# Scan increments from TensorE through diagonal matrices, C rows by DMA, and a staggered end

## The chip, the cores and the metric

The kernel runs on one core of one Trainium2 chip. The metric is the device time of one execution in microseconds (us). Before the change it is 890.41 us, the median of 3 runs (889.49 to 891.13).

## What is computed

Two layers on 4 sequences of 512 tokens and 128 channels. Each layer is an adaptively normalised pair (layer norm, scale and shift from a condition vector, gate on the way back) of an attention part and a feed-forward part. Layer 0 has an additive attention and a feed-forward part with 4-bit block quantisation of activations and weights (width 352). Layer 1 has two stacked state-space (Mamba) layers and a mixture of 8 experts in which each expert picks its tokens. The change lies mostly in the Mamba part:

```python
def _selective_scan(u, dt, A, Bm, Cm, Dvec):
    dA = jnp.exp(dt[..., None] * A)
    dBu = dt[..., None] * Bm[:, :, None, :] * u[..., None]
    def step(h, xs):
        dA_t, dBu_t, C_t = xs
        h = dA_t * h + dBu_t
        y = jnp.einsum('bdn,bn->bd', h, C_t)
        return (h, y)
    ...
    return jnp.swapaxes(ys, 0, 1) + u * Dvec
def _mamba_layer(x, W_in, conv_w, conv_b, W_x, W_dt, b_dt, A_log, Dvec, W_out):
    u, z = jnp.split(jnp.einsum('bld,ed->ble', x, W_in), 2, axis=-1)
    u = _silu(_causal_conv1d(u, conv_w, conv_b))
    dt, Bm, Cm = jnp.split(jnp.einsum('bld,rd->blr', u, W_x), [DT_RANK, DT_RANK + D_STATE], axis=-1)
    dt = jax.nn.softplus(jnp.einsum('blr,dr->bld', dt, W_dt) + b_dt)
    y = _selective_scan(u, dt, -jnp.exp(A_log), Bm, Cm, Dvec) * _silu(z)
    return jnp.einsum('bld,od->blo', y, W_out)
```

Inner width 256 (two chunks of 128 partitions, IC = 2), 16 states (NS), 4 batches (B), 2 Mamba layers (L), all in float32.

## The kernel before

Each engine runs its own program; semaphores order them. Channels lie on the partitions and time along the free dimension, so one scan instruction runs 512 time steps of 2 x 128 channels for one state. The stages in order: attention; the quantised feed-forward part, in 8 pairs of token tiles; layer norm; then for each of the two Mamba layers l a prologue (projection in, convolution, projections to B, C and dt, softplus) and the loop over batches b and states n; back transposition, gate, layer norm and router; the experts.

In the loop, step n of batch b goes through five engines:

- TensorE spreads the C row to all partitions by a matmul with a selecting matrix (`row_sel` times `bc_parts`, the rows as three bf16 parts, L1064), and the B row likewise: into bank `BB` for the 11 states of `NORMAL` (L1075), and three steps ahead into bank `CB` for the 5 states of `SHARE` (L1081).
- ScalarE copies the C row to `c_row` (L766), the B row of a `SHARE` state to `b_row` (L775), and makes the decay exp(dt A) in two activations (L769).
- VectorE multiplies dt u (`dtuT`) by the B row into PSUM for `NORMAL` states (L1453); GpSimd does so into `dbu` for `SHARE` states (L482).
- VectorE scans (L1468): decay times state plus increment.
- GpSimd multiplies the states by the C row (L495) into one of four buffers of `hc`.
- TensorE adds that to the output in banks 0 and 1, as two f32 matmuls with the identity (`add_state`, L1045), three steps behind (`LAG`). Step 8 adds the skip u D (`add_skip`, L1039); step 5 of the next batch projects out (`project_out`, L1051, in layer 1 with the residual, L1055), and ScalarE stores (`store_h`, L756). VectorE gates the output at step 2 of the next batch (`gate_y`, L1441).

Batch 0 is written out and holds the softplus of batches 1 to 3 (L694, L698, L1399) and dt times u (L457); batches 1 to 3 are a hardware loop (`turns`). A f32 matmul is two records of TensorE (MATMUL x2, each with its LDWEIGHTS); a f32 transposition is one.

In the prologue the projection L1030 gives B, C and dt's low rank rows for one batch; L709, L1409, L726, L467 and L468 split B and C in three bf16 parts; L1017 projects dt; L1418 and L737 prepare the softplus.

In the quantised part each pair is divided by its block scales on GpSimd (L394), its magnitude taken on ScalarE (L566), rounded on VectorE in two passes (`round_fp4`, L1264 and L1265), rescaled on GpSimd (L401), transposed (L957) and multiplied (L967); L946 makes gate and up projections.

The end of the last Mamba layer runs one after the other: projection, four times four back transpositions (L1109), gate and addition (L1475, L1479), statistics of all 16 tiles (L1238, L1241), one square root (L786), normalising on VectorE (L1247), transpositions (L1117), modulation (L789), router matmuls (L1122), and the maximum over experts (L1487).

## Time and profile before

| | |
|---|---|
| median of 3 runs | 890.41 us (889.49 to 891.13) |
| the profiled execution | 889.99 us, of which the span from first to last instruction is 888.2 us |
| mean granted TensorE clock | 0.868 of full |
| busy: TensorE, weight loads, VectorE, ScalarE, GpSimd | 71%, 37%, 77%, 49%, 63% of the span |
| stages, us from the span's start | attention to 69; quantised feed-forward to 152; Mamba layer 0: prologue to 204, loop to 437; layer 1: prologue to 480, loop to 714; end and router to 740; choice of tokens to 770; experts to 888 |

TensorE is listed twice, as matmuls (PE) and as weight loads (PEld), which overlap. A matmul's listed duration contains the time in which it drains, while the next one already streams; how much of the engine one takes is read from the distance between starts, which the chain of waits shows as the length of a piece. VectorE is DVE, ScalarE is ACT, GpSimd is POOL, SyncE is SP.

### The profile page before, as it was taken

How to read it: one execution, taken by the hardware profiler on the slowest of the kernel's cores; microseconds unless marked ns; L12 is line 12 of the kernel's file. 1: busy time of each engine (PE TensorE's matmuls, PEld its weight loads, DVE VectorE, ACT ScalarE, POOL GpSimd, SP SyncE). 2: the span in 40 equal slices, each digit the busy share in tenths (PEclk: the TensorE clock that was granted, in tenths of full speed). 3: DMA queues.
4: the chain of work that ended last, by engine and by line, in shares of the span. 5: the costliest groups of instructions: out<-in, count | busy, mean ns of one | idle time of the engine just before them, and what ended most of it. 6: DMA issues, size and time to landing. Idle time of an engine off the chain costs nothing.

```text
span 888.2 us, 8513 instructions
## 1 busy us (share of the span) xinstructions
PE 633.6 (71%) x2393; PEld 327.8 (37%) x2393; DVE 680.2 (77%) x850; ACT 437.8 (49%) x724; POOL 562.2 (63%) x308
## 2 busy tenths in 40 slices
PE   4566765785766877788785767777878745299994
PEld 2253444321322323233221322323323224288883
DVE  6875885678989999999576998999999765934421
ACT  4643332686744655656377755565665423032221
POOL 1336553027988998989414989898989813224446
PEclk9867776875989999999996888999999975599998
DMA  4000000000000000000000000000000071012223
GB/s 169 0 2 1 1 0 1 0 0 1 0 0 1 1 0 0 0 0 0 0 0 1 0 0 1 0 1 0 0 0 0 0 261 48 1 10 22 22 22 25
DMA packets 11633, 13.16 MB, mean 15 GB/s; under 512 B 1336, under 2 KB 9928, under 8 KB 11088
## 3 DMA queue, kind: packets, MB, share of 16 engines
q1 hardware_dynamic: 6912, 10.63, 3.4%
q0 software_dynamic: 4688, 2.13, 2.8%
q8 instruction: 16, 0.26, 0.1%
q14 instruction: 17, 0.14, 0.1%
HBM read 8.51 MB, written 4.23 MB: 14 GB/s over the span
## 4 chain that ended last, share of the span: by engine, by line
PE 35%; DVE 29%; issue 14%; POOL 10%; ACT 8%; DMA 1%; DVEq 1%; POOLq 0%; SPq 0%; ACTq 0%
DVE hs_all L1468 8%; PE ps L1045 7%; DVE ps L1453 6%; POOL hc_all L495 5%; PE ps L1173 3%; PE ps L1207 3%; PE ps L1150 3%; PE ps L1006 3%; ACT ps L769 2%; PE ps L1051 2%; PE ps L946 2%; PE ps L1030 2%; DVE big L1265 2%; DVE dbu L1502 1%; PE ps L1017 1%
## 5 line engine op out<-in xcount | busy, mean ns | idle before, releaser
L1045 PE MATMUL ps<-hc_all,ident 128*128 128x512 f32 x512 | 261.3, 635 | 16.8 <-POOL hc_all L495 15.9
L495 POOL TENSOR_TENSOR hc_all<-hs_all,c_row 128x1024 f32<-128x1024 f32 x88 | 209.0, 2375 | 22.2 <-DVE hs_all L1468 21.7
L766 ACT COPY c_row<-ps 128x512 f32<-128x512 f32 x128 | 74.8, 584 | 162.1 <-PE ps L1064 149.2
L1045 PEld LDWEIGHTS ps<-hc_all,ident 128*128 128x128 f32 x512 | 100.8, 201 | 113.0 <-issue 73.8
L1468 DVE TENSOR_TENSOR_SCAN hs_all<-da,ps 128x1024 f32<-128x1024 f32 x48 | 109.8, 2287 | 13.2 <-ACT da L769 5.5
L769 ACT ACTIVATE da<-big,a_neg 128x511 f32 (+1 forms) x176 | 117.2, 716 | 0.0
L1453 DVE TENSOR_TENSOR ps<-big,ps 128x1024 f32<-128x1024 f32 x88 | 107.3, 1220 | 6.8 <-PE ps L1075 1.5
L495 POOL TENSOR_TENSOR hc_all<-w_ffn,c_row 128x1024 f32<-128x1024 f32 x40 | 94.2, 2355 | 19.8 <-DVE w_ffn L1468 18.5
L482 POOL TENSOR_TENSOR dbu<-big,w_mod 128x1024 f32<-128x1024 f32 x40 | 98.0, 2449 | 0.0
L1468 DVE TENSOR_TENSOR_SCAN hs_all<-ps,dbu 128x1024 f32<-128x1024 f32 x40 | 90.9, 2274 | 7.2 <-POOL hc_all L495 5.8
L1468 DVE TENSOR_TENSOR_SCAN w_ffn<-da,ps 128x1024 f32<-128x1024 f32 x40 | 91.5, 2287 | 5.3
L551 POOL DMA_INDIRECT out<-hc_all,hs_all x32 | 49.4, 1545 | 53.7 <-issue 32.6
L1075 PE MATMUL ps<-bc_parts,row_sel 96*128 (+1 forms) x88 | 36.9, 420 | 58.2 <-DVE ps L1453 58.2
L1064 PE MATMUL ps<-bc_parts,row_sel 96*128 (+1 forms) x128 | 52.8, 413 | 2.2 <-ACT c_row L766 1.5
L467 POOL COPY bc_parts<-hs_all 32x512 bf16<-32x512 bf16 x8 | 4.8, 601 | 75.3 <-ACT hs_all L726 75.1
L769 ACT ACTIVATE ps<-big,a_neg 128x511 f32 (+1 forms) x80 | 52.2, 689 | 0.0
L1075 PEld LDWEIGHTS ps<-bc_parts,row_sel 96*128 96x128 bf16 x88 | 8.7, 99 | 105.9 <-DVE ps L1453 92.3
L820 ACT ACTIVATE big<-ps,b 128x516 f32<-128x516 f32 x32 | 22.1, 690 | 52.1 <-PE ps L1173 52.1
L1428 DVE SCALAR_TENSOR_TENSOR c_row<-hc_all,vecs,c_row 128x512 f32<-128x512 f32 x48 | 37.3, 845 | 11.7 <-ACT c_row L720 11.7
L1081 PE MATMUL ps<-bc_parts,row_sel 96*128 (+1 forms) x40 | 16.4, 410 | 37.8 <-ACT c_row L766 37.8
L946 PE MATMUL ps<-big 128*128 128x352 f32 x64 | 30.7, 644 | 9.0 <-DVE tmpB L1372 6.3
L1527 DVE TENSOR_REDUCE hs_all<-ps 128x4 f32<-128x8 f32 x8 | 1.3, 166 | 42.0 <-PE ps L1156 42.0
(266 smaller groups left out, 1085.7 us busy)
## 6 DMA issues: line engine op xcount, KB each, us to landing
tmpA<-w_in SPq DMA_DIRECT2D x2, 1024.0 KB, 8.1
tmpB<-w_in SPq DMA_DIRECT2D x2, 1024.0 KB, 10.1
x_tok<-x_in SPq DMA_DIRECT2D x2, 512.0 KB, 5.7
out<-x_tok SPq DMA_DIRECT2D x1, 1024.0 KB, 6.9
xm_rows<-xn SPq DMA_DIRECT2D x1, 1024.0 KB, 5.4
w_mod<-w_mod_in SPq DMA_DIRECT2D x2, 384.0 KB, 6.5
w_ffn<-w_ffn_in SPq DMA_DIRECT2D x1, 560.0 KB, 7.8
out<-hc_all,hs_all POOLq DMA_INDIRECT x33, 3.3
```

The costliest lines, as they stand in the source:

```text
L482: nc.gpsimd.tensor_tensor(dbu[:, k, :, :], dtuT[:, b, :, :], b_row[:, k, :].unsqueeze(1).to_broadcast([P, IC, S]), ALU.mult).then_inc(c_in ...
L495: nc.gpsimd.tensor_tensor(hc[:, n % 4, :, :], hs3[HS_BUF[n]].rearrange("p (i s) -> p i s", i=IC), c_row[:, n % 4, :].unsqueeze(1).to_broad ...
L551: nc.gpsimd.indirect_dma_start(out, bass.IndirectOffsetOnAxis(slot_row[:, e, b:b + 1], 0), yg[:, e % 2, b, :], None, compute_op=ALU.add).t ...
L766: nc.scalar.copy(c_row[:, n % 4, :], ps[:, CB, :]).then_inc(c_cs, 1)
L769: ins = nc.scalar.activation(decay, dtT[:, b, i, 1:S], ACT.Exp, scale=a_neg[:, l, i, n:n + 1])
L946: mm = nc.tensor.matmul(ps[:, 1 + 2 * i + j, 0:FF], xqT[:, b % 2, (2 * h + j) * P:(2 * h + j + 1) * P], wgT[:, i, :], start=True, stop=True)
L1045: mm = nc.tensor.matmul(ps[:, YS + i, :], ident[:], hc[:, n % 4, i, :], start=(n == 0), stop=(n == NS - 1))
L1064: nc.tensor.matmul(ps[:, CB, :], row_sel[:, NS + n:NS + n + 1].to_broadcast([96, P]), bc_parts[:, b, :], start=True, stop=True).then_inc(c ...
L1075: nc.tensor.matmul(ps[:, BB, :], row_sel[:, n:n + 1].to_broadcast([96, P]), bc_parts[:, b, :], start=True, stop=True).then_inc(c_bb, 1)
L1428: ins = v.scalar_tensor_tensor(conv[:, b % 2, i, :], u_pad[:, b % 2, i, tap:tap + S], vec(V_CW + (l * IC + i) * KC + tap), conv[:, b % 2, ...
L1453: v.tensor_tensor(ps[:, DBU:DBU + IC, :], dtuT[:, b, :, :], ps[:, BB, :].unsqueeze(1).to_broadcast([P, IC, S]), ALU.mult).then_inc(c_bm, 1)
L1468: v.tensor_tensor_scan(hs3[HS_BUF[n]], decay, step, 0.0, ALU.mult, ALU.add).then_inc(c_scan, 1)
```

## The change

All increments come from TensorE. dt u is transposed to time on the partitions (`turn`, eight f32 transpositions per batch; copied back by ScalarE, `turned`). For every state, B's values of that state, now a column per block of 128 times (`b_cols`), are put on a diagonal (`diagonal` on ScalarE for 11 states, a VectorE multiply of the identity for 5, `DIAG_DVE`), and eight f32 matmuls (2 chunks x 4 time blocks) give the increment in one of two pairs of banks (`increment`). The products on VectorE (L1453) and GpSimd (L482), the bf16 parts, the row broadcasts (L1064, L1075, L1081) and the copies L766 and L775 are gone. C rows are written to memory (`c_rows`) in the prologue and read by SyncE's queue to all partitions, one DMA of 128 x 512 per step, four buffers. The logarithm of the softplus goes to PSUM; batches 0 and 1 have their softplus and dt u before the loop, 2 and 3 within steps 0 to 4. The loop over batches is written out.

The gate of the Mamba output moves into the store of the projection (`ga_cols`), and the end runs batch by batch: back transposition, addition, statistics, square root, normalising (batches 0 and 2 on ScalarE, 1 and 3 on VectorE), transposition, modulation and router of one batch beside those of the others. In the quantised part the magnitudes of the hidden pair go to PSUM and are rounded from there (`round_hidden`), banks are laid out anew, and x is transposed into the gate bank.

```diff
-        bc_parts = sb("bc_parts", [96, B, S], BF16)
-        bc_mid = hs_all[0:2 * NS, 0:S].bitcast(BF16).rearrange("p (k s) -> p k s", k=2)
-        bc_rest = hs_all[0:2 * NS, S:3 * S].rearrange("p (k s) -> p k s", k=2)
+        bc_rows = [hs_all[0:2 * NS, j * S:(j + 1) * S] for j in range(3)] + [hc_all[0:2 * NS, 6 * S:7 * S]]
+        b_cols = sb("b_cols", [P, B, TB, 2 * NS])
...
+        diag = dbu[:].rearrange("p k i (t n) -> p (k i) t n", n=P)
...
-        NORMAL = [n for n in range(NS) if n not in SHARE]
-        ROWS_AHEAD, INC_AHEAD, OUT_AT, Y_AT, SKIP_AT = 3, 3, 5, 2, 8
-        DA_BUF = {n: i % 2 for i, n in enumerate(NORMAL)}
+        DIAG_DVE = [3, 6, 9, 12, 15]
+        DIAG_ACT = [n for n in range(NS) if n not in DIAG_DVE]
+        DIAG_AHEAD, OUT_AT, Y_AT, SKIP_AT = 2, 5, 2, 8
+        TURN_AT = {1: 2, 2: 6, 3: 10}
         HS_BUF = [n % 3 for n in range(NS - 1)] + [1]
...
+        YS, INC, TURN, OUT, IDENT = 0, [2, 4], 4, 6, 7
...
+            for l in range(L):
+                for b in range(B):
+                    sp.wait_ge(sems[l]["m_rows"], b + 1)
+                    sp.dma_start(c_rows[l * B + b, :, :], bc_rows[b][0:NS, :]).then_inc(c_kept, 16)
+                sp.wait_ge(sems[l]["m_u"], IC * B)
+                sp.wait_ge(c_kept, 16 * B * (l + 1))
+                for b in range(B):
+                    for n in range(NS):
+                        after(sp, c_hc, NS * (l * B + b) + n - 3)
+                        sp.dma_start(c_row[:, n % 4, :], c_rows[l * B + b, n:n + 1, :].to_broadcast([P, S])).then_inc(ld_c[n % 4], 16)
...
-                        if n + INC_AHEAD in SHARE:
-                            rows_ready(b, n + INC_AHEAD)
-                        pool.wait_ge(c_cs, at + 1)
+                        pool.wait_ge(ld_c[n % 4], 16 * (NS // 4 * (l * B + b) + n // 4 + 1))
                         after(pool, c_sum, at - 3)
                         pool.wait_ge(c_scan, at + 1)
                         nc.gpsimd.tensor_tensor(hc[:, n % 4, :, :], hs3[HS_BUF[n]].rearrange("p (i s) -> p i s", i=IC),
                                                 c_row[:, n % 4, :].unsqueeze(1).to_broadcast([P, IC, S]),
                                                 ALU.mult).then_inc(c_hc, 1)
-                        if n + INC_AHEAD in SHARE:
-                            increments(b, n + INC_AHEAD)
-                        if isinstance(b, int) and n in DT_AT:
-                            dt_times_u(1 + DT_AT.index(n))
+                        if b == 0 and n in DTU_AT:
...
-                after(act, q_h["q_done"], pair - 1)
-                magnitudes(q_h, pair, hid_flat(pair), mag_h[:, pair % 2, :])
+                after(act, q_h["q_rounded"], pair)
+                magnitudes(q_h, pair, hid[:, pair % 2, :, :], ps[:, MAG:MAG + 2, 0:FF])
...
-                        act.wait_ge(q["m_r1"], b - 1)
-                        after(act, q["m_lo"], b - 3)
-                        nc.scalar.copy(bc_mid[:, k, :], bc_rest[:, k, :]).then_inc(q["m_mid"], 1)
+                        act.wait_ge(b_turn, l * B + b - 1)
+                        nc.scalar.copy(b_cols[:, b - 2, :, :], ps[:, XD[k], 0:P].rearrange("p (t n) -> p t n", t=TB)).then_inc(b_ready, 1)
+                    if b == B + 1:
+                        softplus_ln(1)
...
-                act.wait_ge(decay_zero, l + 2)
+                act.wait_ge(q["m_pos"], IC * (B - 1))
+                nc.scalar.copy(ps[:, IDENT, 0:P], ident[:]).then_inc(c_id, 1)
+
+                def turned(b, i):
+                    act.wait_ge(c_turn, IC * (l * B + b) + i + 1)
+                    nc.scalar.copy(dtuT[:, b, i, :], ps[:, OUT if b else TURN + i, :]).then_inc(c_turned, 1)
+
+                def diagonal(b, n):
+                    after(act, c_inc, NS * (l * B + b) + n - 3)
+                    for t in range(TB):
+                        ins = nc.scalar.activation(diag[:, n % 4, t, :], ident[:], ACT.Identity, scale=b_cols[:, b, t, NS + n:NS + n + 1])
+                    ins.then_inc(c_dga, 1)
+
+                turned(0, 0)
+                turned(0, 1)
+                act.wait_ge(b_ready, (l + 1) * B)
+                act.wait_ge(decay_zero, 1)
                 act.wait_ge(a_ready, 1)
...
+                        after(act, c_scan, at - 1)
                         for i in range(IC):
-                            decay = ps[:, DAP + i, 1:S] if n in SHARE else da[:, DA_BUF[n], i, 1:S]
-                            ins = nc.scalar.activation(decay, dtT[:, b, i, 1:S], ACT.Exp, scale=a_neg[:, l, i, n:n + 1])
+                            ins = nc.scalar.activation(da[:, n % 2, i, 1:S], dtT[:, b, i, 1:S], ACT.Exp, scale=a_neg[:, l, i, n:n + 1])
                         ins.then_inc(c_da, 1)
-                        if n + ROWS_AHEAD in SHARE:
-                            m = n + ROWS_AHEAD
-                            act.wait_ge(c_cb, ROWS * (l * B + b) + rows_before(n) + 2)
...
+            act.preload_act_table(ACT.Sqrt)
+            deviation(0)
+            normalise_tiles(0, 3)
+            deviation(1)
+            store_h(B)
+            modulated_again(0)
+            deviation(2)
+            normalise_tiles(2, 4)
+            deviation(3)
+            modulated_again(1)
+            modulated_again(2)
+            modulated_again(3)
...
+                        pe.wait_ge(q["m_rows"], b - 1)
+                        for t in range(TB):
+                            mm = nc.tensor.transpose(ps[:, XD[b % 2], t * 2 * NS:(t + 1) * 2 * NS], bc_rows[b - 2][:, t * P:(t + 1) * P],
+                                                     ident[0:2 * NS, 0:2 * NS])
+                        mm.then_inc(b_turn, 1)
...
+                def turn(b, i):
+
+                    pe.wait_ge(q["m_dtu"], b + 1)
+                    if b == 0:
+                        pe.wait_ge(b_ready, (l + 1) * B)
...
+                    for t in range(TB):
+                        mm = nc.tensor.transpose(ps[:, OUT if b else TURN + i, t * P:(t + 1) * P], dtuT[:, b, i, t * P:(t + 1) * P], ident[:])
+                    mm.then_inc(c_turn, 1)
+
+                def increment(b, n):
+
+                    at = NS * (l * B + b) + n
+                    if n == 0:
+                        pe.wait_ge(c_turned, IC * (l * B + b + 1))
+                        if b == 0:
+                            pe.wait_ge(q["m_dt"], 2)
+                    after(pe, c_scan, at - 1)
+                    if n in DIAG_ACT:
+                        pe.wait_ge(c_dga, diags(DIAG_ACT, l * B + b, n))
+                    else:
+                        pe.wait_ge(c_dgv, diags(DIAG_DVE, l * B + b, n))
+                    for i in range(IC):
+                        for t in range(TB):
+                            mm = nc.tensor.matmul(ps[:, INC[n % 2] + i, t * P:(t + 1) * P], dtuT[:, b, i, t * P:(t + 1) * P],
+                                                  diag[:, n % 4, t, :], start=True, stop=True)
+                    mm.then_inc(c_inc, 1)
...
+                        increment(b, n)
...
+            transposed_again(0)
+            back(3)
+            route(0)
+            for i in range(1, B):
+                transposed_again(i)
+                route(i)
...
+            def round_hidden(pair):
+                dve.wait_ge(q_h["q_divided"], pair + 1)
+                dve.wait_ge(q_h["q_mag"], pair + 1)
+                buf, mag = hid[:, pair % 2, :, :], ps[:, MAG:MAG + 2, 0:FF]
+                rounded = mag_h[:, pair % 2, :].rearrange("p (t f) -> p t f", t=2)
+                chain.link(v.scalar_tensor_tensor(buf, mag, ROUND_LOW, buf, ALU.max, ALU.add))
+                v.scalar_tensor_tensor(rounded, mag, ROUND_LOW, buf, ALU.max, ALU.subtract).then_inc(q_h["q_rounded"], 1)
...
+                        m = n + DIAG_AHEAD
+                        if m in DIAG_DVE:
+                            if m == DIAG_DVE[0] and b == 0:
+                                dve.wait_ge(c_id, l + 1)
+                            after(dve, c_inc, NS * (l * B + b) + m - 3)
+                            v.tensor_tensor(diag[:, m % 4, :, :], ps[:, IDENT, 0:P].unsqueeze(1).to_broadcast([P, TB, P]),
+                                            b_cols[:, b, :, NS + m:NS + m + 1].to_broadcast([P, TB, P]), ALU.mult).then_inc(c_dgv, 1)
                         dve.wait_ge(c_da, at + 1)
+                        dve.wait_ge(c_inc, at + 1)
                         after(dve, c_hc, at - HS_SINCE[n] + 1)
-                        if n in NORMAL:
...
+            add_mamba(0)
+            inverse(0, True)
+            gate_y(B)
+            add_mamba(1)
+            add_mamba(2)
+            inverse(1, False)
+            inverse(2, True)
+            add_mamba(3)
+            normalise_again(1)
+            inverse(3, False)
+            normalise_again(3)
```

## Rows read from the trace of the kernel before

**Rows 1.** The page's busy time, share of the span and instructions per engine

```profile
PE 633.6 (71%) x2393; PEld 327.8 (37%) x2393; DVE 680.2 (77%) x850; ACT 437.8 (49%) x724; POOL 562.2 (63%) x308
```

**Rows 2.** Busy us by stage: window; PE, PEld, DVE, ACT, POOL; clock; DMA share; GB/s

```profile
285.00:338.20 53.20, 41.62 (x105) 16.72 (x105) 50.41 (x28) 32.08 (x54) 49.05 (x22) 0.97 0.00 0
...
613.00:667.00 54.00, 43.82 (x106) 17.60 (x106) 50.52 (x29) 32.09 (x54) 49.20 (x22) 0.94 0.00 0
```

**Rows 3.** Timeline of a steady step: start us, us, engine, line, operation, out<-in

```profile
302.79 1.33 ACT L769 ACTIVATE da<-big,a_neg 128x511 f32 x2
...
303.27 1.21 DVE L1453 TENSOR_TENSOR ps<-big,ps 128x1024 f32<-128x1024 f32 x1
303.66 2.36 POOL L495 TENSOR_TENSOR hc_all<-hs_all,c_row 128x1024 f32<-128x1024 f32 x1
...
304.61 2.29 DVE L1468 TENSOR_TENSOR_SCAN hs_all<-da,ps 128x1024 f32<-128x1024 f32 x1
...
305.98 2.39 POOL L482 TENSOR_TENSOR dbu<-big,w_mod 128x1024 f32<-128x1024 f32 x1
```

**Rows 4.** Chain of waits in the loop: start us, length us, what

```profile
276.78 0.07 DVE y_sb L1441
...
289.16 1.72 PE ps L1051 x4
290.88 0.22 PE ps L1081
...
348.42 1.72 PE ps L1045 x4
```

**Rows 5.** Chain of waits among the experts

```profile
782.99 2.68 PE ps L1150 x48
787.71 3.68 PE ps L1207 x32
...
799.78 5.31 PE ps L1207 x32
...
861.71 1.92 PE ps L1190 x16
```

**Rows 6.** Timeline of the first steps of layer 0's loop

```profile
204.37 1.23 DVE L1453 TENSOR_TENSOR ps<-big,ps 128x1024 f32<-128x1024 f32 x1
...
206.82 2.29 DVE L1468 TENSOR_TENSOR_SCAN hs_all<-da,ps 128x1024 f32<-128x1024 f32 x1 [1.23 <-ACT da L769]
...
216.41 3.62 PE L1045 MATMUL ps<-hc_all,ident 128*128 128x512 f32 x4
```

**Rows 7.** Timeline of one pair of the quantised feed-forward part

```profile
101.06 0.89 DVE L1264 SCALAR_TENSOR_TENSOR tmpB<-big,tmpB 128x704 f32<-128x704 f32 x1
101.23 1.96 POOL L394 TENSOR_TENSOR tmpB<-tmpB,q_inv 128x704 f32<-128x704 f32 x1 [2.81 <-DVE q_inv L1257]
...
101.98 1.96 DVE L1265 SCALAR_TENSOR_TENSOR big<-big,tmpB 128x704 f32<-128x704 f32 x1
...
103.98 1.64 ACT L635 ACTIVATE big<-x_tok,nmr,rstd 128x128 f32<-128x128 f32 x4
```

**Rows 8.** Timeline from the last gate to the router

```profile
710.84 1.22 DVE L1441 TENSOR_TENSOR y_sb<-ps,tmpB 128x1024 f32<-128x1024 f32 x1 [4.59 <-PE ps L1045]
...
715.64 1.97 PE L1109 MATMUL ps<-ident,xn 128*128 128x128 f32 x16 [0.68 <-ACT xn L756]
716.34 0.69 DVE L1475 TENSOR_TENSOR dbu<-ps,gates 128x512 f32<-128x512 f32 x1 [4.27 <-PE ps L1109]
...
721.77 3.19 DVE L1238 BATCH_NORM_STATS2 stats<-x_tok 128x6 f32<-128x128 f32 x16
...
726.69 4.19 DVE L1247 TENSOR_SCALAR xn<-x_tok,mv,rstd 128x128 f32<-128x128 f32 x16
...
732.92 7.00 PE L1122 MATMUL ps<-w_router,hT 128*128 128x8 f32 x32 [0.87 <-ACT hT L789]
```

**Rows 9.** DMA issues: out<-in, queue, count, KB each, median us to landing

```profile
y_sb<-b_in SPq DMA_DIRECT2D x1, 512.0 KB, 12.3
```

346 lines of the change are left out of this document (158 added, 188 removed).

## The prediction, made before the change was run

> **What bounds the kernel now.** I read the busy table first [rows 1]: no engine is near 100%, VectorE leads with 77%, and the change touches mainly the two scan loops. So the table by stage came next [rows 2]. In a steady batch of 16 state steps, 53.2 us, VectorE is busy 50.4 us, GpSimd 49.1, TensorE 41.6, ScalarE 32.1. One step shows why [rows 3]: VectorE runs a scan of 2.29 us and, in 11 of 16 steps, a multiply of 1.21 us; 16 x 2.29 + 11 x 1.21 + one gate of 1.22 = 51.2 us. GpSimd has 16 products of 2.36 and five of 2.39, 49.7 us. The two are almost tied, and the period is 53.2 / 16 = 3.33 us.
>
> TensorE's busy time overstates its occupation, since a matmul's duration contains its drain. What occupies it is its start-to-start distance, and the chain of waits gives that: one state addition (L1045, two f32 matmuls of 512 columns, four records) goes by in 1.72 us, the skip (L1039), of the same shape, likewise, a projection (L1051) in 1.72, a row broadcast (L1081, and so the others) in 0.22 [rows 4]. So a steady batch occupies TensorE for 16 x 1.72 + 2 x 1.72 + 32 x 0.22 = 38.0 us of 53.2. It has some 15 us to spare per batch, and that is what the change spends.
>
> **The change in the loop.** Removed per step: VectorE's multiply, GpSimd's five products per batch, ScalarE's copy of the C row and all row broadcasts. Added per step: eight f32 matmuls of 128 columns, each with its own weights (a block of dt u transposed against a diagonal block of B), and a diagonal of 128x512 made by ScalarE (11 of 16) or VectorE (5 of 16).
>
> The matmul's price decides. The same shape exists in the expert outputs, L1207: f32, 128x128 weights, 128 columns, new weights each time. There 16 matmuls are 32 records and take 3.68 us from start to start at the full clock [rows 5], 0.115 us a record. An increment is 16 records, so 16 x 0.115 = 1.84 us. From below, the pure streaming share of the 512-column matmul is 1.72 / 4 / 4 = 0.1075 us for 128 columns, 1.72 us an increment; from above, L1190, such weights with 4 columns, takes 1.92 / 16 = 0.12 us a record [rows 5], 1.92 us. I take 1.84, the identical shape.
>
> TensorE per step is then 1.84 + 1.72 = 3.56 us, and per batch 16 x 3.56 + 1.72 (skip) + 1.72 (projection) = 60.4 us; layer 1 adds the residual matmul, half of 1.72, so 61.3. The others fall behind. VectorE: 16 x 2.29 + 1.22 + 5 diagonals. A diagonal there has one PSUM operand; the nearest row is L1475, 128x512 from PSUM, 0.69 us [rows 8]; from above stands the all-SBUF pass beside a busy GpSimd, 1.96 for 704 columns, 1.43 for 512 [rows 7]: 41.3 to 45.0 us. GpSimd 16 x 2.36 = 37.8. ScalarE: 16 exponentials of 1.33 and 11 diagonals; four 128x128 activations took 1.64 us [rows 7], so 39.3 us. None of these reaches 60, so they cost nothing while TensorE is dense. The increment waits for the scan two steps back, which has started 5.3 us (1.72 + 1.84 + 1.72) before and needs 2.3; it also waits for its diagonal, which ScalarE makes about two steps ahead. Behind it in TensorE's queue stand the state additions, with three steps of lag. I see no wait that would bite in the steady part.
>
> Steady batches therefore get 60.4 - 53.2 = 7.2 us longer in layer 0 and 8.1 us in layer 1. Batch 0 is different. Today it takes from the first multiply at 204.4 to the gate at 276.8, 72.4 us, as the softplus of three batches and three dt u products lie in it [rows 4, 6]. After the change, four increments come out slowly (below), and then TensorE owes 19 increments, 16 additions, the skip and 24 transposes (16 such took 1.97 [rows 8], so 3.0 us) until the same gate: 35.0 + 27.5 + 1.7 + 3.0 = 67.2 us, plus the 6 us of the slow start. That is a draw. Loops as a whole: +21.6 us in layer 0, +24.3 in layer 1. Clock: steady batches had a granted clock of 0.94 and 0.97 [rows 2], an L1045 group at the 1.2 GHz level took 3.62 instead of 1.72 us [rows 6]. Denser work should keep 2.4 GHz; I add 1 us per loop for a start at the lower level. Sum for the loops +48, rounded.
>
> **C rows by DMA.** 128 copies of a 2 KB row, 256 KB per step, issued when the product four steps earlier is done, so with 4 x 3.56 - 2.36 = 11.9 us to land. Nearest row: 512 KB behind four megabytes landed after 12.3 us [rows 9], itself about at that limit, but twice the size and with a full queue ahead, while 256 KB per 3.56 us is 74 GB/s on engines that are idle here (DMA share 0.00, [rows 2]). No row shows a source that all partitions share. I take zero, and keep the other end as a rival. SyncE does nothing else in the loops; what stands behind its 128 issues, the expert weights, is issued after the last gate at 710.8 and is used by the experts shortly before 783 today [rows 5, 8]; the end gets some 14 us shorter, so cover stays.
>
> **Before each loop.** Removed: the split of B and C in three bf16 parts (small copies and subtractions on 32 partitions). Added: four small transposes after each dt projection (0.12 us each by [rows 8], twice that at the slow clock) and a copy. The wait for them stands in ScalarE ahead of the silu of the next batch, so in two of four rounds it lengthens the chain, by about 1 us each. Larger is the new tail: after the last dt projection come the softplus of batches 0 and 1, dt u (a GpSimd product, 2.36 as in [rows 3]), then eight transposes, two copies of about 0.6, a diagonal of 1.64 [rows 7], an increment at the slow clock (twice 1.84) and only then the first scan; today there is one multiply and one exponential. Counted through, with ScalarE as the thread, the first scan moves from 206.8 [rows 6] to 217, +10; where ScalarE's pieces overlap better, +6. I take +9 in each layer, +18.
>
> **Quantised feed-forward.** VectorE's second rounding pass over 704 columns takes 1.96 us while GpSimd divides beside it, the first 0.89 [rows 7]; in the loop the multiply with a PSUM operand keeps its 1.21 beside a GpSimd product [rows 3]. The change reads the magnitudes from PSUM, so 1.07 us less per pair. But in the middle pairs the chain goes through TensorE (L946, L967, L957), and only the lone pairs, three, and part of the three double ones see it: 3 x 1.07 + 3 x 0.4 = 4.4; bounds 1 (the new wait for the previous rounding eats it) and 8.6 (every pair). Taken -4.
>
> **The end.** Today from the gate at 710.84 to the end of routing, 732.92 + 7.00 = 739.92: 29.1 us [rows 8]. In it lie the projection, the copy, 16 transposes, four gatings of 0.68 and four additions, statistics of all 16 tiles (3.19 and the aggregation), normalising (4.19), modulation and 7.00 us of routing. After: three batches are done before or during the last projection. What remains behind the gate for batch 3, by quarters of those rows and estimates from the neighbouring small operations: gate 1.3, projection 2.8, copy 0.65, transposes 0.8, addition 0.7, statistics 1.1, root and reciprocal 0.8, normalising batches 1 and 3 (half of 4.19) 2.1, transposes 0.8, modulation 0.8, routing 1.75, and routing of batch 1 ahead of it in TensorE's queue 1.75: 15.4. So -13.7.
>
> **Sum.** Profiled execution 889.99: -4 + 18 + 48 - 13.7 = +48.3, which is 938. The median of the runs, 890.41, is 0.4 above the profiled one, so 938 or 939; I say 938.
>
> A rule that speaks against my price: the Trainium skill, "TensorE: Matmul & The Clock Gate", section on the back-to-back issue gap, states for a sustained stream of weight load and matmul pairs about 81 ns each at 128 columns. The section names no type; for 16 records it would be 1.30 us. This case's trace does not agree for f32, with 115 ns.
>
> **Rivals.** (A) TensorE bound as summed: 938. For: VectorE's and GpSimd's loads drop by 8 to 12 us a batch while TensorE gets 60.4. (B) TensorE bound and dearer: handoffs between increment and addition, or dips of the clock. Evidence: an L1207 group of 32 took 5.31 instead of 3.68 [rows 5]. One such dip per batch is 8 x 1.7 = 14 us, and 0.1 us at each step's handoff 13 more: 965. Against: today a broadcast follows the projection at once, 289.16 + 1.72 = 290.88 [rows 4]. (C) TensorE bound and cheaper: 0.12 us less per step (the lower bound), 15 us, and prologues at +6: 938 - 15 - 6 = 917. (D) The other side, faster than before: the increment's records pass well under L1207's pace. The place is the TensorE queue in each step; it decides from 48.3 / 128 = 0.38 us less per step, 1.46 us an increment, 92 ns a record. At the pace of the bf16 gather, L1150, 2.68 / 48 = 0.056 us [rows 5], an increment is 0.90 and a batch 16 x 2.62 + 3.44 = 45.4, 7.8 less than now; 890 - 4 + 18 - 62 - 13.7 = 828. Against it: three f32 shapes in this trace agree on 107 to 120 ns. At the pace of the Trainium skill's page named above a batch would be 51.8 and the whole about 879; the same rows speak against it. (E) The C rows come late. It decides from 11.9 us; if one takes 16 with four in flight, a step is (16 + 2.36) / 4 = 4.6 us, 1.03 more than 3.56 in each of 128: 1070. Against: DMA queues are empty in the loops.
>
> **How the numbers follow.** A 0.65, B 0.17, C 0.10, D 0.04, E 0.04. Prediction 938. (Of D, half goes to the pace that the named page of the Trainium skill would give.) The unknowns of A (increment 1.72 to 1.92: -15 to +10; prologues -6 to +3; feed-forward -4.6 to +3; end 3 either way), not all on one side at once, give about 920 to 954. The range takes in B and C: 914 to 966; D and E, 8 in 100, stay out with the far ends. A measurement of this kernel tells 0.2% from no change; D lies wholly below, so faster 0.04, same 0.01, slower 0.95.
>
> **What would show it.** In the trace after: TensorE with almost no idle time in batches 1 to 3 and a period of 60 to 61 us; 16 records of an increment in about 1.84 us; VectorE idle before each scan, released by TensorE; GpSimd idle before its products, released by the scan and never by the DMA; VectorE's rounding at 0.9 us; router scores about 15 us after the last gate; first scan about 10 us later in its stage. It would be wrong if increments took under 1.5 or over 2.1 us, if the C rows released GpSimd, or if instructions of the unrolled loops came late, which today's straight expert code does not show.

## The result, and the profile after

The changed kernel takes 922.86 us, the median of four runs (921.51 to 924.88), against 890.27 for the kernel before beside it on the same chip: a ratio of 1.0368, 95% interval 1.0346 to 1.039. The profiled execution took 921.51 us, with a span of 919.8. (One run of the shared increments, further down, took 1085.58 us at a mean granted clock of 0.62 and is left out of that experiment's ratio.)

From the page after: busy time per engine, the chain that ended last, and the line of the granted TensorE clock (tenths, 40 slices of the span).

```profile
PE 782.5 (85%) x4283; PEld 545.3 (59%) x4283; DVE 566.1 (62%) x785; ACT 467.5 (51%) x938; POOL 445.5 (48%) x248
PEclk9768885968999999999996899999999996599997
PE 76%; DVE 11%; ACT 7%; POOL 2%; issue 2%; DMA 1%; POOLq 0%; SPq 0%; DVEq 0%; ACTq 0%
PE ps L1097 24%; PE ps L1059 24%; PE ps L1220 3%; PE ps L1254 3%; PE ps L1019 3%; PE ps L1197 3%; PE ps L1030 2%; PE ps L1065 2%; PE ps L858 2%; PE ps L1053 1%; PE ps L960 1%; DVE dbu L1565 1%; PE ps L1047 1%; DVE top L1564 1%; PE ps L981 1%
```

Against [rows 1] TensorE went from 71% to 85%, VectorE from 77% to 62%, GpSimd from 63% to 48%. The increment (L1097) and the state addition (L1059) are half of the chain.

The stages, in the columns of [rows 2]: a steady batch of each layer, batch 0 of layer 0 from the first scan to its gate, and the end from the last gate to the router's scores.

```profile
286.80:346.56 59.76, 59.75 (x330) 42.21 (x330) 40.43 (x23) 34.57 (x79) 37.66 (x17) 1.00 0.23 71
583.40:644.00 60.60, 60.59 (x332) 42.57 (x332) 40.42 (x23) 34.64 (x79) 37.69 (x17) 1.00 0.22 70
753.00:772.30 19.30, 14.56 (x67) 10.98 (x65) 10.04 (x41) 8.34 (x16) 2.60 (x9) 0.70 0.82 300
...
212.65:279.56 66.91, 65.35 (x382) 48.34 (x381) 46.61 (x27) 46.32 (x100) 46.95 (x20) 0.99 0.24 67
```

TensorE is busy 59.75 of 59.76 us; no other engine reaches 41. Two steps in the chain of waits (compare [rows 4]), and in the timeline of a step who waits for whom:

```profile
332.27 1.79 PE ps L1097 x16
334.06 1.72 PE ps L1059 x4
335.77 1.78 PE ps L1097 x16
337.56 1.72 PE ps L1059 x4
```

```profile
330.65 2.29 DVE L1512 TENSOR_TENSOR_SCAN hs_all<-da,ps 128x1024 f32<-128x1024 f32 x1 [1.22 <-PE ps L1097]
...
332.85 0.67 DVE L1505 TENSOR_TENSOR dbu<-ps,b_cols 128x512 f32<-128x512 f32 x1
...
333.10 2.36 POOL L461 TENSOR_TENSOR hc_all<-hs_all,c_row 128x1024 f32<-128x1024 f32 x1 [1.15 <-DVE hs_all L1512]
```

An increment takes 1.785 us (16 records of 0.1116), an addition 1.718, a step 3.503. The scan waits 1.22 us for the increment, GpSimd for the scan. 16 x 3.503 + 1.72 (skip) + 1.72 (projection) = 59.5 us, the period less 0.3.

Where the time went, from the two traces. A gate is the VectorE multiply L1441 before, L1490 after; its four starts in a layer divide the loop.

| Stretch | before, us | after, us | difference | predicted |
|---|---|---|---|---|
| to the statistics after the quantised part | 152.20 | 150.37 | -1.8 | -4 |
| prologue of layer 0, to the first scan | 54.6 | 62.3 | +7.7 | +9 |
| layer 0, first scan to first gate | 69.96 | 66.91 | -3.1 | 0 (+1 clock) |
| layer 0, the two periods between gates 1, 2, 3 | 53.2, 53.0 | 59.8, 59.8 | +13.2 | +14.4 |
| layer 0, gate 3 to gate 4 | 50.4 | 54.5 | +4.0 | +7.2 |
| prologue of layer 1, gate 4 to the first scan | 48.4 | 55.8 | +7.4 | +9 |
| layer 1, first scan to first gate | 69.9 | 66.8 | -3.1 | 0 (+1 clock) |
| layer 1, the two periods | 53.9, 53.9 | 60.6, 60.6 | +13.5 | +16.2 |
| layer 1, gate 3 to gate 4 | 51.3 | 55.7 | +4.4 | +8.1 |
| last gate to the router's scores | 29.1 | 19.2 | -9.9 | -13.7 |
| choice of tokens and experts | 148.3 | 147.5 | -0.8 | 0 |
| sum | 888.2 | 919.8 | +31.5 | +48.3 (the rows give 48.2; the loops had been rounded up) |

### The profile page after: what moved, and what is told of

Its sections match the earlier page's. It is cut to its first block, busy times and chain, and to the rows that moved or that the text cites. A ratio compares the mean times of both kernels' runs of the same rounds, so it can differ in the third digit from the quotient of the medians.

```text
span 919.8 us, 11465 instructions
## 1 busy us (share of the span) xinstructions
PE 782.5 (85%) x4283; PEld 545.3 (59%) x4283; DVE 566.1 (62%) x785; ACT 467.5 (51%) x938; POOL 445.5 (48%) x248
## 4 chain that ended last, share of the span: by engine, by line
PE 76%; DVE 11%; ACT 7%; POOL 2%; issue 2%; DMA 1%; POOLq 0%; SPq 0%; DVEq 0%; ACTq 0%
PE ps L1097 24%; PE ps L1059 24%; PE ps L1220 3%; PE ps L1254 3%; PE ps L1019 3%; PE ps L1197 3%; PE ps L1030 2%; PE ps L1065 2%; PE ps L858 2%; PE ps L1053 1%; PE ps L960 1%; DVE dbu L1565 1%; PE ps L1047 1%; DVE top L1564 1%; PE ps L981 1%
## 5 line engine op out<-in xcount | busy, mean ns | idle before, releaser
L1097 PEld LDWEIGHTS ps<-dbu,big 128*128 128x128 f32 x2048 | 252.2, 196 | 66.6 <-issue 58.4
L1512 DVE TENSOR_TENSOR_SCAN hs_all<-da,ps 128x1024 f32<-128x1024 f32 x88 | 201.0, 2284 | 108.3 <-PE ps L1097 75.5
L1097 PE MATMUL ps<-dbu,big 128*128 128x128 f32 x2048 | 255.3, 280 | 10.7 <-ACT dbu L728 8.0
L755 ACT ACTIVATE da<-big,a_neg 128x511 f32<-128x511 f32 x256 | 170.4, 713 | 164.1 <-DVE hs_all L1512 124.9
L1059 PE MATMUL ps<-hc_all,ident 128*128 128x512 f32 x512 | 240.2, 593 | 0.0
L1059 PEld LDWEIGHTS ps<-hc_all,ident 128*128 128x128 f32 x512 | 87.9, 191 | 63.7 <-issue 62.8
L728 ACT ACTIVATE dbu<-ident,b_cols 128x128 f32<-128x128 f32 x352 | 110.4, 387 | 0.0
L515 POOL DMA_INDIRECT out<-hc_all,hs_all x32 | 49.4, 1544 | 51.3 <-issue 31.5
L1254 PE MATMUL ps<-tmpB,big 128*128 128x128 f32 x256 | 32.6, 287 | 0.8 <-ACT big L833 0.8
L1254 PEld LDWEIGHTS ps<-tmpB,big 128*128 128x128 f32 x256 | 31.0, 200 | 1.4 <-ACT big L833 1.2
L1220 PE MATMUL ps<-hc_all,tmpA 128*128 128x258 f32 x128 | 30.7, 388 | 0.5 <-DVE hc_all L1597 0.5
L1505 DVE TENSOR_TENSOR dbu<-ps,b_cols 128x512 f32<-128x512 f32 x40 | 26.7, 667 | 0.0
L1220 PEld LDWEIGHTS ps<-hc_all,tmpA 128*128 128x128 f32 x128 | 22.4, 190 | 6.4 <-ACT big L833 2.5
```

Source lines behind the costliest of these rows:

```text
L515: nc.gpsimd.indirect_dma_start(out, bass.IndirectOffsetOnAxis(slot_row[:, e, b:b + 1], 0), yg[:, e % 2, b, :], None, compute_op=ALU.add).t ...
L728: ins = nc.scalar.activation(diag[:, n % 4, t, :], ident[:], ACT.Identity, scale=b_cols[:, b, t, NS + n:NS + n + 1])
L755: ins = nc.scalar.activation(da[:, n % 2, i, 1:S], dtT[:, b, i, 1:S], ACT.Exp, scale=a_neg[:, l, i, n:n + 1])
L1059: mm = nc.tensor.matmul(ps[:, YS + i, :], ident[:], hc[:, n % 4, i, :], start=(n == 0), stop=(n == NS - 1))
L1097: mm = nc.tensor.matmul(ps[:, INC[n % 2] + i, t * P:(t + 1) * P], dtuT[:, b, i, t * P:(t + 1) * P], diag[:, n % 4, t, :], start=True, stop ...
L1220: mm = nc.tensor.matmul(ps[:, HH + 2 * (at % 2) + g, 0:GRP], w1[:, e, c * P:(c + 1) * P], xg[:, e % 2, g * GRP:(g + 1) * GRP], start=True, ...
```

## Experiments

Theory: in the loops TensorE's own records are the bound, two f32 matmul forms of 1.785 and 1.718 us per step, and the other engines, the C rows and the hand-overs are covered. The rivals were the round of one step (increment, scan, product, addition) with TensorE only looking full, the C rows, and the clock. The kernel before was timed with every group of kernels; its median was 887.8 us beside the first four below, 895.1 beside the shared increments, the balanced diagonals and the undone end, 894.1 beside the undone rounding and the filled gap, 891.0 beside the last. So totals are compared by the ratio to it, and stretches by the traces.

### Half of the increment's matmuls

```diff
-                    for i in range(IC):
+                    for i in range(1):
                         for t in range(TB):
```

> Half of the increment's matmuls are left out (those of the second group of 128 inner channels), so part of the computation is missing. Theory 1, TensorE's own work is the bound: a step costs TensorE 1.79/2 + 1.72 = 2.61 us where it cost 3.50, and the next engine, VectorE, has 2.29 for the scan and a third of 0.67 for a diagonal = 2.5 us; so about 2.65 us a step, 128 times 0.85 = 109 us less: about 814 us (805 to 830), with TensorE still above 95% busy in a steady batch. Rival, the round of one step (increment, scan, product, addition, buffers coming free) is the bound and TensorE only looks full: the scan still waits for the same chain, and the total stays above 900 us.

Measured: 819.2 us, in one run. A steady batch, in the columns above:

```profile
313.02:359.38 46.36, 45.72 (x202) 27.96 (x201) 39.94 (x22) 34.20 (x78) 37.71 (x17) 1.00 0.28 91
```

59.76 - 46.36 = 13.4 us a batch for 16 x 8 records fewer, 0.84 us a step where 0.89 left TensorE's queue. TensorE is still busy 99%. The rival with the round of one step is out.

### bf16 increments

```diff
-        diag = dbu[:].rearrange("p k i (t n) -> p (k i) t n", n=P)
+        diag = dbu[:].rearrange("p k i s -> p (k i s)").bitcast(BF16)[:, 0:4 * S].rearrange("p (k t n) -> p k t n", k=4, n=P)
+        dtu16 = big[:, IC * T:2 * IC * T].bitcast(BF16).rearrange("p (b i s) -> p b i s", b=B, i=IC)
...
-                    nc.scalar.copy(dtuT[:, b, i, :], ps[:, OUT if b else TURN + i, :]).then_inc(c_turned, 1)
+                    nc.scalar.copy(dtu16[:, b, i, 0:S], ps[:, OUT if b else TURN + i, :]).then_inc(c_turned, 1)
...
-                            mm = nc.tensor.matmul(ps[:, INC[n % 2] + i, t * P:(t + 1) * P], dtuT[:, b, i, t * P:(t + 1) * P],
+                            mm = nc.tensor.matmul(ps[:, INC[n % 2] + i, t * P:(t + 1) * P], dtu16[:, b, i, t * P:(t + 1) * P],
```

> The increment's two operands are kept as bf16, so the increment is rounded and its matmuls leave one record instead of two; the state additions stay f32. Theory 1, the price of the f32 matmul makes TensorE the bound: an increment takes 8 records of about 0.056 us = 0.45 us in place of 1.79, a TensorE step 2.17 us, below VectorE's 2.5 and GpSimd's 2.36; so VectorE is the bound again, about 2.6 us a step: 805 to 820 us, TensorE idle for 15% or more of a steady batch. Rival, the hand-over between the engines or the C rows bounds the loop: the total stays above 890 us.

Measured: 783.45 us, in one run, below the range that I had written. The chain of waits, and a steady batch:

```profile
322.22 0.45 PE ps L1098 x8
322.67 1.77 PE ps L1060 x4
324.44 0.45 PE ps L1098 x8
324.88 1.77 PE ps L1060 x4
```

```profile
263.22:304.07 40.85, 39.73 (x200) 19.85 (x200) 39.32 (x24) 34.09 (x77) 37.40 (x16) 1.00 0.33 104
```

Eight records take 0.45 us, 0.056 each: an increment in f32 is 16 records of 0.112, and that difference is more than the whole loss of the change. (Its operands and diagonals are half as large too; everything else is as in the changed kernel.) My total was wrong by its arithmetic: I took 0.9 us off each of 128 steps of 3.50, but a batch is 59.8 us long, its 3.4 us of skip and projection included, and 40.9 is 18.9 less, not 14. That VectorE was the bound now also fell, below (the balanced diagonals).

The Trainium skill's "TensorE: Matmul & The Clock Gate", section "Back-to-back issue gap", gives 81 ns for a sustained pair of weight load and matmul at 128 columns and, by its formula for a single one, about 56. In this trace eight pairs in bf16 follow each other at 56 ns, and in f32 a matmul is two pairs at 112 ns each, 223 ns together; the 81 ns fit neither.

### Every C row read twice

```diff
+                        sp.wait_ge(ld_mod[0], 16 * (NS * (l * B + b) + n + 1))
+                        sp.dma_start(spare[n % 4], c_rows[l * B + b, n:n + 1, :].to_broadcast([P, S])).then_inc(ld_mod[0], 16)
```

> Each of the 128 reads of a C row to all partitions is made twice, the second one to tiles that nobody reads. Theory 1, the reads are hidden (3.1 us to landing where about 11.9 are there): no change, ratio to the changed kernel within 0.2%, 921 to 925 us. Rival, the reads take part in setting the loop, by the traffic into memory of the partitions or by the queue: with 33 MB more in the loops the time grows by over 5 us, to 928 or more.

Measured: 922.85 us, ratio 1.0391 (1.0372 to 1.0411) beside 1.0368 of the changed kernel. The page of the changed kernel and then of this one, DMA issues (columns of [rows 9]):

```profile
c_row<-c_rows SPq DMA_DIRECT2D x128, 256.0 KB, 3.1
```

```profile
c_row<-c_rows SPq DMA_DIRECT2D x128, 256.0 KB, 3.3
```

The gates are 59.76 and 60.62 us apart, as without the second read. Twice the traffic (141 GB/s in a steady batch where it was 71) raises a read by 0.2 us and costs the loop nothing. The C rows are out as a cause, with a reserve: 3.1 us to landing, where 4 x 3.50 - 2.36 = 11.6 us are there.

### Two orders on TensorE

```diff
-                after(pe, f_x, pair)
+                after(pe, f_x, min(pair, 2 * B - 2))
...
-                        mm = nc.tensor.matmul(ps[:, HIDT + j, 3 * P:4 * P], hqT[0:n, pair % 2, j, k, :],
+                        mm = nc.tensor.matmul(ps[:, DOWN.get(pair, HIDT) + j, 3 * P:4 * P], hqT[0:n, pair % 2, j, k, :],
...
             for i in range(1, B):
                 transposed_again(i)
+            for i in range(1, B):
                 route(i)
```

> Two orders on TensorE. (a) In the drain of the quantised part the last two down projections go to free banks, so that the transposes of the last hidden pair needn't wait for the addition of the pair before: theory, this wait costs 2.1 us (the drain took 11.9 us where it took 9.75 before the change). (b) In the end, the three later transposes stand before the three routings rather than in turn with them: theory, 1.3 us, as the routing of one batch no longer holds up the next batch's transposes. Sum: 3.4 us less, 919.5 us (918 to 921). Rival, both waits are covered by other work (the additions of VectorE in the drain, the copies and statistics in the end): within 1 us of the changed kernel, 922 to 924.

Measured: 920.97 us, ratio 1.0382 (1.0364 to 1.04), so no gain that the totals show. The traces show both gains where they were expected, and what ate one. In the drain, chain of waits of the changed kernel, then of this one:

```profile
140.96 2.95 PE ps L981 x12
...
143.93 0.43 DVE x_tok L1412
...
144.50 1.53 PE ps L972 x6
...
146.95 2.94 PE ps L981 x12
```

```profile
141.74 2.93 PE ps L985 x12
144.66 1.29 PE ps L973 x6
...
146.88 1.62 PE ps L985 x12
```

With the free banks the transposes follow the down projection at once, and the drain takes 9.6 us (139.35 to 148.98) instead of 11.9. The wait itself is only 0.6 of these 2.3 us. The larger part, 1.3 us, is the last down projection, the same twelve records in 2.94 us at a granted clock of 0.50 and in 1.62 us at 1.00. TensorE stood idle ahead of it for 0.6 and 0.9 us in the changed kernel and once for 0.9 us here; that this set the level is not shown. The end takes 17.3 us instead of 19.2. But in the prologue of layer 1 one stretch of the projection L1019, the same eight matmuls, took 5.33 instead of 3.63 us; the windows of that stage, first of the changed kernel, then of this one:

```profile
465.00:480.00 15.00, 13.42 (x35) 4.89 (x36) 9.44 (x14) 11.43 (x20) 0.00 (x0) 1.00 0.02 5
```

```profile
465.00:480.00 15.00, 13.67 (x33) 4.76 (x31) 7.91 (x12) 9.86 (x16) 0.00 (x0) 0.89 0.02 5
```

The granted clock was 0.89 there in place of 1.00, and that took 1.7 us back. The kernel with doubled reads had the same dip (0.89) and the same 1.7 us. So a gain of 2 us can be lost to where such a dip falls. What puts it there is not shown: each trace is one execution, on one of several chips, and from the last gate of layer 0 to the first scan of layer 1 the kernels of this document with the changed prologue took between 54.0 and 57.5 us.

### Increments shared between VectorE and TensorE

```diff
-        DIAG_DVE = [3, 6, 9, 12, 15]
+        ROWS_DVE = [1, 3, 5, 7, 9, 11, 13, 15]
...
+                            v.tensor_tensor(ps[:, INC[n % 2]:INC[n % 2] + IC, :], dtuT[:, b, :, :],
+                                            ps[:, BB, :].unsqueeze(1).to_broadcast([P, IC, S]), ALU.mult).then_inc(c_bm, 1)
...
-                        increment(b, n)
+                        if n in DIAG_ACT:
+                            increment(b, n)
```

> The increments are shared in f32: the eight odd states are multiplied by VectorE again (a B row is read to all partitions by DMA and copied to PSUM by ScalarE), the eight even ones stay with TensorE's diagonals, all made by ScalarE. Theory 1, each engine's own work adds up and the larger sum is the period: TensorE 8 x 1.785 + 16 x 1.718 + 3.44 = 45.2 us a batch, VectorE 16 x 2.28 + 8 x 1.21 + 1.22 = 47.4; so VectorE at about 48.5 us in place of 59.8 and 60.6, eight batches, 90 us less than the changed kernel: 833 us (825 to 845). Rival, TensorE and VectorE now take turns in every second step and hand-overs cost more than is saved: steady batches above 52 us, total above 860.

> The shared increments of e5 and the two orders of e4 together. Theory 1: the two gains are independent, so 2 us below e5, about 831 us, the fastest of the versions with f32 increments. Rival, the end or the drain is covered differently when the loop is no longer bound by TensorE: within 1 us of e5.

Measured: 841.1 us, ratio 0.9391 (0.9332 to 0.9451), and with the orders 837.0 us, 0.9357 (0.9306 to 0.9407). A steady batch of each layer in the first of the two:

```profile
314.77:363.10 48.33, 46.81 (x208) 28.43 (x208) 46.11 (x26) 35.96 (x76) 37.53 (x17) 1.00 0.41 132
571.53:620.72 49.19, 47.66 (x210) 28.80 (x210) 46.16 (x25) 35.97 (x76) 37.57 (x17) 1.00 0.39 128
```

48.3 and 49.2 us where I had 48.5: the sums of the engines add up, with 1 to 2 us lost where TensorE and VectorE are nearly tied. The total is higher than 833, since the first batch of a loop gained 12 and the last 8 us instead of 11 each, and the kernel before was itself 0.5% slower beside it. The second kernel is the best f32 version here, 6.4% faster than the kernel before, with half as many diagonals of the same kind. The two orders' 0.4% lies inside the intervals.

### bf16 increments with fewer diagonals on VectorE

```diff
-        DIAG_DVE = [3, 6, 9, 12, 15]
+        DIAG_DVE = [5, 10, 15]
```

The cut shows the new edit; those of the bf16 increments and of the two orders come with it.

> The bf16 increments of e2 (dt u transposed and the diagonals rounded to bf16), the two orders of e4, and three diagonals of a batch by VectorE where there were five, the other thirteen by ScalarE. Theory 1, VectorE alone is the bound with bf16 increments: e2's steady batch of 40.8 us is 16 x 2.27 + 1.21 + 5 x 0.67 = 40.9; with three diagonals 39.5, while ScalarE comes to 16 x 1.33 + 13 x 1.26 = 37.7; eight batches by 1.3 us are 11, the orders 2: 783 - 13 = 770 us (766 to 776). Rival, ScalarE's work per step or the round through GpSimd (2.36 a step, 37.8 a batch) is as binding as VectorE: 778 or more.

Measured: 785.0 us, ratio 0.877 (0.8726 to 0.8814). By the ratios that is 0.6% less than the bf16 kernel without it (783.45 / 887.84 = 0.8824, from its one run), and the period did not move:

```profile
299.84:340.81 40.97, 39.68 (x201) 20.05 (x202) 38.59 (x21) 36.02 (x87) 37.42 (x16) 1.00 0.33 103
```

VectorE lost 0.7 us of work and the period stayed (40.82 us before the edit, 40.97 now). The theory that VectorE alone bounds the bf16 loop fell. The chain of waits tells the bound: from the third step on it is TensorE alone, 0.45 + 1.77, and at the batch's start it goes through two scans of VectorE. The timeline has what holds the first addition there, the gate:

```profile
300.98 2.29 DVE w_ffn L1518
...
303.32 0.53 PE ps L1102 x7
303.84 2.20 DVE hs_all L1518
...
306.09 0.62 PE ps L1102 x8
306.71 1.77 PE ps L1064 x4
```

```profile
301.12 1.98 PE L1064 MATMUL ps<-hc_all,ident 128*128 128x512 f32 x4 [0.69 <-DVE y_sb L1496]
```

16 x 2.22 + 3.44 = 39.0 us, and about 2 us at the batch's start. There TensorE stands idle for 0.69 us until the gate has freed the sum's banks, and for 0.21 and 0.38 us until the scans that stand behind the gate on VectorE are done. In the bf16 kernel without this edit the chain of such a batch was on TensorE from 307.5 to 329.3 us and then, up to 345, mostly on VectorE's scans and ScalarE's decays and diagonals. So VectorE had been one of several bounds that lie close together. The state additions are now the larger part of TensorE's work. Both bf16 kernels are some 6% faster than the best f32 one, at the price of increments rounded to bf16.

### The end's overlap undone

```diff
-                    if l and n == NS - LAG:
-                        pe.wait_ge(c_scan, NS * L * B - 1)
-                        back(0)
-                if l:
-                    back(1)
...
-                    back(2)
...
                 project_out(B - 1)
+                if l:
...
+                    for b in range(B - 1):
+                        back(b)
```

> The changed kernel with the overlap of its end undone: the last batch's gate and projection come first, and transposing back, addition, statistics and normalising of batches 0 to 2 start only after them; the per-batch order of the rest stays. Theory 1: VectorE has 4 x (0.69 + 0.87 + 0.36) = 7.7 us of additions and statistics behind the projection in place of 1.9 behind it, so the routing ends 5 to 6 us later, 24.5 instead of 19.2 us after the last gate: 928 us (926.5 to 930). Rival, the serial stretch of normalising, transposing and routing on TensorE sets the end alone, and the early batches gain nothing: under 924.5 us.

Measured: 929.0 us, ratio 1.038 (1.0327 to 1.0433), an interval too wide to tell 5 us in the total; the trace tells them. The last gate is at 753.30, the scores are ready at 777.88: 24.6 us, as expected. So of the 9.9 us that the end gained, 5.4 come from doing three batches early. The other 4.5 are left to the rest of the end's edits (the order batch by batch, the gate inside the store, normalising on two engines), which no run takes apart. What is left is serial; the chain of waits of the changed kernel, for one of its batches:

```profile
764.86 0.96 PE ps L1155 x4
765.82 0.02 issue
765.84 0.79 ACT hT L789
766.63 0.04 issue
766.67 1.88 PE ps L1162 x8
768.55 0.96 PE ps L1155 x4
```

Transposing (0.96), modulation (0.79) and routing (1.88) of one batch end before the next begins, 3.7 us for each of three. Over these three the granted clock is 0.50 (0.70 is the mean of the whole end); batch 0's transposes and routing, ahead of them at 1.00, took 0.60 and 1.06 us.

### The rounding's place undone

```diff
-                magnitudes(q_h, pair, hid[:, pair % 2, :, :], ps[:, MAG:MAG + 2, 0:FF])
+                magnitudes(q_h, pair, hid[:, pair % 2, :, :], mag_h[:, pair % 2, :].rearrange("p (t f) -> p t f", t=2))
...
-                buf, mag = hid[:, pair % 2, :, :], ps[:, MAG:MAG + 2, 0:FF]
+                buf, mag = hid[:, pair % 2, :, :], mag_h[:, pair % 2, :].rearrange("p (t f) -> p t f", t=2)
```

> Of the quantised part's edits only the place of the magnitudes is undone: ScalarE writes them to SBUF again, and both rounding passes of VectorE read and write SBUF alone. Theory: the second pass takes 1.96 instead of 0.90 us beside a working GpSimd, and GpSimd's product that runs beside it 1.96 instead of 1.39; a lone pair then takes 8.0 instead of 6.9 us and a double pair about 20.1 instead of 19.3, so 3 x 1.1 + 3 x 0.8 = 5.7 us more: 928.5 us (926 to 930.5). Rival, the passes are covered by TensorE and ScalarE, and the gain came from the order: under 924.5.

Measured: 931.4 us, ratio 1.0411 (1.0387 to 1.0435), 0.4% above the changed kernel's ratio. The second rounding pass, in the chain of waits, of the changed kernel and then of this one:

```profile
129.13 0.90 DVE big L1312
130.03 0.07 issue
130.10 1.39 POOL tmpB L393
```

```profile
133.82 1.97 DVE big L1312
135.79 0.07 issue
135.86 1.40 POOL tmpB L393
```

Everything up to the last hidden transposes comes 7.5 us later (145.98 against 138.48), more than the 5.7 that I expected. The two double pairs take 21.6 and 20.8 us (hidden transposes to hidden transposes), where they took 19.5 and 19.7 in the changed kernel and 20.1 and 20.3 in the kernel before, so the new order alone is no gain there. GpSimd's division beside the rounding takes 1.96 instead of 1.39 us. In the last pair GpSimd does nothing beside the second pass, and the pass takes 0.89 us with its magnitudes in SBUF. The Trainium skill's "SBUF — State Buffer", section "Who interferes with whom", says that a VectorE instruction with two SBUF inputs contends with a GpSimd instruction that reads SBUF; the 1.97, 0.90 and 0.89 us of the same pass agree.

### The clock at the start of each loop

```diff
                 turn(0, 1)
+                for k in range(14):
+                    nc.tensor.matmul(ps[:, OUT, 0:P], ident[:], ident[:], start=True, stop=True)
                 pe.wait_ge(diag_ready, 1)
```

> Ahead of each layer's first increment TensorE stands idle for 3.9 us and then runs three increments at the granted clock 0.50 (48 records in 8.34 us). Here 14 idle matmuls of 128 columns, whose result nobody reads, fill that gap. Theory 1, the low level comes from the idle time just before: the increments run at 2.4 GHz, the first one 1.9 us sooner, and as VectorE is dense right behind it, about 2 us a layer are saved: 919 us (917.5 to 920.5). Rival 1, the level comes from the thin work of the last stage as a whole, and 3 us of work don't lift it: the increments still take 2.8 us each, no change, 921 to 924.5, or slightly more where the fill runs past the gap.

Measured: 927.8 us, ratio 1.0378 (1.0361 to 1.0395): nothing gained, though the clock did rise. Windows of the changed kernel, and then of this one, in the columns of [rows 2]:

```profile
208.70:212.70 4.00, 3.94 (x18) 3.97 (x19) 0.05 (x1) 4.00 (x11) 0.00 (x0) 0.50 0.00 0
```

```profile
208.70:212.70 4.00, 4.00 (x34) 4.00 (x34) 0.00 (x0) 4.00 (x12) 0.00 (x0) 0.88 0.00 0
```

The first two increments now took 3.74 us at a granted clock of 1.00. But the fill ran half a microsecond past the gap, the first scan came only 1.3 us sooner after the transposes of dt u, and the first gate came 68.2 us after it instead of 66.9: measured from those transposes (202.81 and 204.69), both kernels reach the first gate after 76.75 us. ScalarE is busy 4.00 of 4.00 us in both windows. It makes the diagonals, the decays and the softplus of two more batches one after the other, and the chain of waits stays with it for 17.8 us in both kernels (204.94 to 222.73 and 206.83 to 224.62). So ScalarE holds the start.

> The filled gap of e10 (12 idle matmuls instead of 14), and the softplus of batches 2 and 3 with their dt u one step later, so that ScalarE makes the decay of state 1 before it. In e10 the increments ran at 2.4 GHz and the loop gained nothing. Theory, the start of each loop hangs on ScalarE, not on TensorE: the softplus (2.1 us on ScalarE) stands ahead of the second decay and so of the second scan; with it moved the second scan comes about 2 us sooner and TensorE is dense from there: first scan to first gate 65 to 66 us instead of 66.9 (the changed kernel) and 68.2 (e10). Rival, ScalarE's and VectorE's sum over the first five steps counts and not its order: the first gate stays 68 us behind the first scan, and the total stays at e10's ratio of 1.038 to the kernel before.

```diff
-        DTU_AT = {1: 2, 4: 3}
+        DTU_AT = {2: 2, 5: 3}
...
-                        if b == 0 and n < 2:
-                            softplus_exp(2 + n)
-                            softplus_ln(2 + n)
+                        if b == 0 and 0 < n < 3:
+                            softplus_exp(1 + n)
+                            softplus_ln(1 + n)
...
```

Measured: 928.8 us, ratio 1.0429 (1.0406 to 1.0453), worse than either case. The timeline says why:

```profile
213.19 2.29 DVE L1514 TENSOR_TENSOR_SCAN hs_all<-da,ps 128x1024 f32<-128x1024 f32 x1 [5.63 <-ACT da L755]
...
215.97 2.27 DVE L1514 TENSOR_TENSOR_SCAN hs_all<-da,ps 128x1024 f32<-128x1024 f32 x1
...
223.13 3.53 PE L1059 MATMUL ps<-hc_all,ident 128*128 128x512 f32 x4 [2.77 <-DVE big L1456]
```

The second scan stands 2.8 us behind the first (4.6 with the gap filled, 3.9 in the changed kernel), so the order on ScalarE does count. But the first addition waits for the last softplus, whose logarithm lies in the banks of the sum; TensorE stood idle for 2.77 us and then ran at half its pace (3.53 for 1.72, at a granted clock of 0.54), and the gate is 70.1 us behind the first scan. What would be gained with the logarithm in other banks is open; it wasn't tried.

## Why the prediction was right, and where its steps were off

Forecast 938 in 914 to 966, measured 922.86: the direction and the range hold, and case A is what happened: TensorE at 59.75 of 59.76 us. The halved, the shared and the bf16 increments show the mechanism, for the loops got shorter with each as TensorE's work did. The number lies nearer to case C (917, put at 0.10) than to A's 938, since nearly all of the error is in the loops and on one side. Against the profiled executions the sum was 16.8 us too high: loops 19, prologues 3 and the rest 1 too dear, the quantised part 2 and the end 4 too cheap.

- The price of the matmul. 0.1116 us a record, against 0.115 taken from the expert outputs [rows 5] and 0.1075 as the lower bound. Steady batches were to be 60.4 and 61.3 and are 59.76 and 60.6: 0.65 us for each of six, 4 us. The nearest row was good to 3%.
- Layer 1's base. I set 8.1 us against a period of 53.2, while [rows 2] has 54.0 for layer 1: 61.3 - 54.0 is 7.3. Three times 0.8 is 2.4 us.
- The last batch of a layer. I gave it the full difference. Between the third and the fourth gate TensorE has no increments of a next batch to make, three of 1.785 = 5.4 us, and the stretch is 54.5 us; in the kernel before, the same place was shorter by 2.7 alone. 2 x 2.6 = 5 us. The prediction counted a period from the first batches and multiplied by three without looking at the last.
- Batch 0. "A draw", at 73.2 us against 72.4. Measured 70.8 from the first increment at 208.76 to the gate, and 66.9 from the first scan, 3.1 less than before, twice: 6 us. The slow start was added to 19 increments that already held it, and one of these lies ahead of the first scan: 18 x 1.785 + 16 x 1.718 + 1.72 + 2.7 (24 transposes) = 64.0, and 1.6 us of idle TensorE and about 1 of the low clock give the rest. In this sum the low clock has a place, but raising it brought the gate no sooner (the filled gap), since ScalarE holds the first 18 us.
- Clock, +2 for the loops: 1.00 in steady batches, nothing lost. The kernel before had 0.97 and 0.94 there [rows 2].
- The prologues. +7.7 and +7.4 where +9 stood, inside the +6 to +10 written. That ScalarE is the thread was right: from 204.94 us past the first scan at 212.65 the chain is on it.
- The quantised part. The part up to the last hidden transposes gained 4.0 us, the forecast. But a down projection now shares a bank pair with the hidden transposes, which brings a wait (`after(pe, f_x, pair)`) ahead of them; in the drain nothing covers it. With the down projection at the low clock behind it, it goes with 2.3 us. The wait stood in the diff, and I didn't list it.
- The end. -9.9 for -13.7. Gate, projection and statistics were sized well, but the last batch's addition and statistics are not on the chain: behind the copy it goes to the deviation and normalising of batch 2 on ScalarE, so the first of the last transposes comes 7.9 us after the gate, where the sum has 10.3. Behind that I counted the serial part of one batch and a routing ahead of it, 5.1 us. Three batches go through transposing, modulation and routing in turn there, 11.3 us, at a granted clock of 0.50.
- C rows taken at zero: right, 3.1 us to landing; the rival E had no ground.

Case D, the faster side, decided from 1.46 us an increment. The bf16 experiment measures 0.45 and lands at 783 us, so its mechanism was sound and only f32 kept it away. (The 92 ns a record of that case lie between the two measured prices, 56 and 112.)

## What to carry to other kernels

Before work goes to an engine with idle time, add up what occupies that engine per period in the matmul form that it will really use: here f32 meant twice the records at twice the time each, and moving eleven increments and five products broke a tie between VectorE and GpSimd only to make TensorE a dearer bound. A split near the point where the two sums meet (8 of 16 states) was 9.4% faster than moving all (0.9391 / 1.0368), and 6% faster than the kernel before. A period read from the steady part holds neither for the first nor for the last batch of a loop. Every new wait in a diff is to be looked at in the drain, too: there nothing hid it. And before a dip of the clock is mended, see which engine holds the chain in that stretch.
